# Attention rows 0 and 1: their scores made together in the step of row 2, side by side in the four score banks

## The reference

```python
q = (x_norm @ w_q.T).reshape(B, 512, 16, 32)      # 16 heads of 32
k, v = split(x_norm @ w_kv.T)                     # one key and one value head for all
q, k = rotary(q * scale), rotary(k * scale)
attn = einsum('bnih,bjh->bnij', q, k)             # causal: j <= i
out = einsum('bnij,bjd->bind', softmax(attn), v)
x = x + out.reshape(B, 512, 512) @ w_proj.T + b_proj
```

## Time and profile before

| | us |
|---|---|
| median of 3 runs | 2768.08 (2767.12 to 2768.15) |
| the profiled execution, its own time | 2771.93 |
| its span, first to last instruction | 2769.9 |
| mean granted TensorE clock | 0.994 |
| TensorE busy (share of the span) | 2718.5 (98%) |
| VectorE busy | 1852.0 (67%) |
| ScalarE busy | 1122.9 (41%) |
| GpSimd busy | 305.5 (11%) |

### The profile page before, as it was taken

The page is one execution under the profiler, slowest core; times in us unless marked ns, Lnnn a source line. Parts: engine busy times, 40 slices in busy tenths (PEclk is TensorE's granted clock), DMA queues, the critical chain, the costliest instruction groups (busy, mean ns, idle before and its releaser), DMA issues.

```text
span 2769.9 us, 41675 instructions
## 1 busy us (share of the span) xinstructions
PE 2718.5 (98%) x15520; PEld 2196.0 (79%) x15520; DVE 1852.0 (67%) x3533; ACT 1122.9 (41%) x2399; POOL 305.5 (11%) x316
## 2 busy tenths in 40 slices
PE   7999999999999999999999999999999999999998
PEld 5888888888888887677777768888888888888887
DVE  5667666765675667777777775667656766676555
ACT  3333333333333323777777774333333333333331
POOL 0000000000000004444444420000000000000000
PEclk9999999999999999999999999999999999999999
DMA  3210311131112111000000012211221032112100
GB/s 118 87 61 24 127 56 45 39 114 46 45 62 91 46 46 57 21 13 28 32 32 28 28 47 92 81 48 47 79 81 63 28 118 66 45 33 89 46 15 31
DMA packets 65069, 156.49 MB, mean 56 GB/s; under 512 B 6784, under 2 KB 7040, under 8 KB 64640
## 3 DMA queue, kind: packets, MB, share of 16 engines
q1 hardware_dynamic: 64896, 154.17, 16.5%
HBM read 128.97 MB, written 25.17 MB: 56 GB/s over the span
## 4 chain that ended last, share of the span: by engine, by line
PE 94%; DVE 4%; ACT 1%; POOL 1%; issue 1%; ACTq 0%; DVEq 0%; POOLq 0%
PE bank L371 50%; PE bank L392 24%; PE bank L1003 5%; PE bank L971 3%; PE bank L994 3%; PE bank L1018 3%; PE bank L1031 2%; PE bank L273 1%; DVE probs L1254 1%; PE bank L946 1%; PE bank L979 1%; POOL xnt_l L875 0%; DVE att L1273 0%; ACT hs_h L486 0%; DVE stats L243 0%
## 5 line engine op out<-in xcount | busy, mean ns | idle before, releaser
L371 PE MATMUL bank<-xnt_h,wgu_h 128*128 128x512 f32 x2048 | 803.0, 392 | 6.6 <-issue 3.7
L371 PE MATMUL bank<-xnt_h,wgu_l 128*128 128x512 f32 x2048 | 798.4, 390 | 0.0
L371 PE MATMUL bank<-xnt_l,wgu_h 128*128 128x512 f32 x2048 | 798.1, 390 | 0.0
L539 DVE TENSOR_TENSOR h<-bank,sg 128x512 f32<-128x512 f32 x256 | 176.8, 690 | 592.6 <-PE bank L371 577.0
L371 PEld LDWEIGHTS bank<-xnt_h,wgu_h 128*128 128x128 f32 x2048 | 385.1, 188 | 87.2 <-issue 5.1
L476 ACT ACTIVATE mag<-h 128x512 f32<-128x512 f32 x256 | 161.9, 633 | 713.5 <-DVE h L539 713.5
L371 PEld LDWEIGHTS bank<-xnt_h,wgu_l 128*128 128x128 f32 x2048 | 385.1, 188 | 80.9
L371 PEld LDWEIGHTS bank<-xnt_l,wgu_h 128*128 128x128 f32 x2048 | 385.3, 188 | 78.7
L392 PE MATMUL bank<-wd_h,hs_h 128*128 128x512 f32 x1024 | 399.6, 390 | 4.6 <-DVE hs_l L574 4.6
L392 PE MATMUL bank<-wd_l,hs_h 128*128 128x512 f32 x1024 | 399.3, 390 | 0.0
L392 PE MATMUL bank<-wd_h,hs_l 128*128 128x512 f32 x1024 | 399.2, 390 | 0.0
(11 more groups left out here) (109 smaller groups left out, 3195.8 us busy)
## 6 DMA issues: line engine op xcount, KB each, us to landing
raw_gu<-in_w_gu SPq DMA_DIRECT2D x128, 512.0 KB, 4.9
raw_d<-in_w_d SPq DMA_DIRECT2D x128, 256.0 KB, 2.6
x_mid<-x_sb SPq DMA_DIRECT2D x64, 256.0 KB, 2.0
x_sb<-x_mid SPq DMA_DIRECT2D x10, 1024.0 KB, 5.5
x_sb<-in_x SPq DMA_DIRECT2D x32, 256.0 KB, 4.8
out<-x_sb SPq DMA_DIRECT2D x32, 256.0 KB, 2.1
x_sb<-x_mid SPq DMA_DIRECT2D x24, 256.0 KB, 5.0
raw_q<-in_w_q SPq DMA_DIRECT2D x1, 1024.0 KB, 5.2
```

The costliest lines, as they stand in the source:

```text
L371: last = pe.matmul(ps, w[:, r, kind, k], xs[:, b, k], start=(i == 0), stop=(i == 3 * KD - 1))
L539: v.tensor_tensor(h[:, r], bank[UP + r % 2][:, :], sg[:, r % 2], ALU.mult).then_inc(h_done, 1)
```

## The change

Row 0's scores are no longer made in the step of row 1. They are made in the step of row 2, just ahead of those of row 1, and both lie in the same four banks at once: row 0 in columns 0 to 127, row 1 in columns 128 to 383. Row 1 does not wait for row 0 to be masked. One semaphore step of two announces both. The step of row 1 makes no scores. VectorE masks all heads of row 0 at the end of its step of row 2 (behind invert_sums) in place of the start of that step; ScalarE makes all four exponentials of row 0 at the end of its step of row 3, behind its two copies of turned blocks. The scores made before the first step (rows 0, 1 and 2 of the first head group) keep their order.

```diff
+            def columns(i):
+                first = P if i == 1 else 0
+                return slice(first, first + width(i))
 # TensorE
-                def scores(K):
+                def scores(K, beside=False):
...
-                    if K > 0:
+                    if K > 0 and not (beside and i == 1):
                         pe.wait_ge(masked, K * HG)
...
-                        last = pe.matmul(bank[SCORES + s][:, 0:width(i)], qt[rows, B % 2, hg, i * P:(i + 1) * P],
+                        last = pe.matmul(bank[SCORES + s][:, columns(i)], qt[rows, B % 2, hg, i * P:(i + 1) * P],
...
-                    last.then_inc(score_done, 1)
+                    if not beside:
+                        last.then_inc(score_done, 1)
+                    elif i == 1:
+                        last.then_inc(score_done, 2)
...
-                    if K + AHEAD < ALL:
+                    if i == 2 and K + AHEAD < ALL:
+                        scores(K + AHEAD - 1, beside=True)
+                        scores(K + AHEAD, beside=True)
+                    elif i != 1 and K + AHEAD < ALL:
                         scores(K + AHEAD)
 # ScalarE
-                    exps(K + 1, 2)
+                    if row_of(K) != 3:
+                        exps(K + 1, 2)
                     copy_turned(K, 0)
-                    exps(K + 1, 3)
+                    if row_of(K) != 3:
+                        exps(K + 1, 3)
                     if 2 in mine:
                         copy_turned(K, 2)
...
-                    exps(K + 2, 0)
-                    exps(K + 2, 1)
+                    if row_of(K) == 3:
+                        for s in range(HG):
+                            exps(K + 1, s)
+                    if row_of(K) != 2:
+                        exps(K + 2, 0)
+                        exps(K + 2, 1)
 # VectorE
-                    mask_scores(K + AHEAD - 1, (0, 1))
+                    if i != 2:
+                        mask_scores(K + AHEAD - 1, (0, 1))
                     if 1 in ON_VECTOR[i]:
                         copy_turned(K, 1)
-                    mask_scores(K + AHEAD - 1, (2, 3))
+                    if i != 2:
+                        mask_scores(K + AHEAD - 1, (2, 3))
...
-                    if k % TT == TT - 2:
+                    if i == 2:
                         invert_sums(K // TT)
+                        mask_scores(K + AHEAD - 1, range(HG))
```

More of the change, by code:

```diff
@@ L1253, in mask_scores @@
                     for s in heads:
-                        v.tensor_tensor_reduce(out=probs[:, K % 3, s, 0:w], in0=bank[SCORES + s][:, 0:w], in1=causal[:, S - w:S],
+                        v.tensor_tensor_reduce(out=probs[:, K % 3, s, 0:w], in0=bank[SCORES + s][:, columns(row_of(K))], in1=causal[:, S - w:S],
                                                scale=1.0, scalar=MASKED, op0=ALU.add, op1=ALU.min,
```

## The result

The changed kernel takes 2778.84 us (median of 5 runs, 2778.23 to 2779.37), the kernel before beside it 2767.12 (5 runs, 2763.04 to 2768.15). The ratio is 1.0043, 95% interval 1.0032 to 1.0055: slower by 11.7 us. The prediction was 2778 (2769 to 2788) with 0.73 for slower by over 0.2%.

A forecast was written before the change was run, and what follows sets the result against it. TensorE's queue bounds the kernel, with VectorE late in the row 3 step. Six middle batches +13.0, ends -1.3 and -3.5, a low-clock stretch +1.7: +9.9 us, 2781.8 profiled; less 3.9, 2778 us (2769 to 2788).

The forecast's parts named there:

- The row 3 step: From T, the start of its turns, to row 2's scores: 3.11 us, not 2.57, as VectorE masks row 0 first; +0.54.
- The price of the pair: Row 0's scores put ahead of row 1's on TensorE cost 0.22 us more in one group; upper bound 0.43.
- Rival (e): The merged score group costs 0.43 us, not 0.22: +6, 2784 us; inside the range, no chance of its own.
- The swallowed saving: In k = 5 to 6 the 0.52 us saved becomes TensorE's wait for the projection bank that VectorE frees.
- k = 9 to 12: Head group where VectorE's normalise and ScalarE's drain delay TensorE: +0.98 and +0.34 among terms summing to +0.89 us.
- Rival (d): ScalarE becomes the bound, row 1's last exponential 0.4 us before TensorE in k=8; each 0.1 beyond costs 1.5 us.
- k = 13 to 0: Head group ending each batch: -0.41 us saved, +0.16 from ScalarE's late row 0 exponentials in k=15; together -0.25.
- The ends: First and last batch: TensorE's waits for row 0's place in the banks go; -1.3, -3.5, and +1.7 for a low-clock stretch.
- The -4.4 of batch 0: Batch 0, from the start of k = 9 to the turns of k = 11: 5.73 us in place of 10.15.
- (a): Row 0's masks fit into VectorE's slack, so the row 3 step costs nothing: 2756 us; chance 0.08.
- (b): It comes out even: no loss in k=12, and the ends give more without a clock stretch: 2771 us; chance 0.19.
- (c): New or longer waits in k=1, 5, 12 let the clock fall: 2798 us, or 2788 for one per batch; chance 0.11.

The follow-up runs named there:

- run 5: Changed kernel with two extra 128-column VectorE copies among row 0's four masks, results unread: 2784.81 us, ratio to the kernel before 1.0073.
- run 8: Changed kernel with weigh placed between row 0's and row 1's score groups, same matmuls, waits and banks: 2785.05 us, ratio to the kernel before 1.0072.
- runs 1 to 3: Changed kernel with normalise ahead of row 0's masks (2779.45 us), with row 0's exponentials split around the copy of block 0 (2773.78), with both (2771.43).
- run 4: Kernel before with only ScalarE's new order of row 0's exponentials: 2783.51 us, ratio to the kernel before 1.0061.
- the two later ones: Second and third profiles of the unchanged kernel before: 2767.59 and 2766.62 us; attention stretch 573.3 and 573.1 us, against 575.8 in the first.
- runs 1 to 8: The follow-up variants timed in five rounds beside the kernel before, whose median was 2767.85 us beside the first four and 2767.18 beside the others.
- run 2: Changed kernel with row 0's exponentials on ScalarE split around the copy of block 0: 2773.78 us, ratio to the kernel before 1.0023.

## Why the prediction was right, and where it was not

**The row 3 step** is where the time goes, as predicted: T + 3.10 in the trace, 3.11 in the sum, and the extra copies of run 5 (0.41 of VectorE's queue) made each such step 0.40 longer. k = 1 to 4 and 5 to 8: +0.75 and +0.78 in batch 3 against +0.76.

**The price of the pair**: 0.22, measured 0.22, and run 8 shows that it hangs on the two groups being neighbours: parted, row 0's costs 0.21 more. The Trainium skill gives a reason (TensorEngine Tiling (Array Packing), Key Properties: a change of tiling mode drains TensorE, a change of tile does not). The 0.21 fit it, but no run parts the drain from another cost of starting a group, so the reason is argued and not shown. Rival (e) falls.

**The swallowed saving**: shown in the trace (0.80 of wait for the bank of the projection in k = 6), the start unchanged relative to the projection before.

**k = 9 to 12**: +0.97 in all in batch 3, summed as +0.89. The wait of k = 12 was a little longer than summed (0.43 of delay against 0.34). What runs 1 to 3 add is that these are two bounds in a row, and run 4 that ScalarE's new order by itself costs a middle batch as much as the whole change. Rival (d) was put as a risk of ScalarE in k = 8; the place where it bites is the drain of k = 12.

**k = 13 to 0**: -0.36 against -0.25. **A batch**: 2.15 on the mean against 2.16, six of them 12.9 against 13.0.

**The ends** were mis-sized, and by two errors that partly cancel. Against the first trace they gave 1.7 (batch 0) and 2.6 (batch 7), 4.3 in all, where the sum had 1.3 + 3.5 - 1.7 = 3.1. But 2.5 of that is the low stretch that the first trace had and the two later ones had not. The step that went wrong is "it lies 3.9 above the median ... so for the runs I say 2778": it took the 3.9 for something that both kernels keep. Most of it was a low stretch in the very place that the change rebuilds; the profiled run of after lies 0.5 above its median. With 2.5 less to win at the end the attention of after is 11.2 us longer than that of before, and the timed runs say 11.7, not the 9.9 of the sum. The landing within 1 us of the time is partly luck; the sum of the middle is not.

The -4.4 of batch 0 came out (T of k = 11 at 5.57 after the start of k = 9, summed as 5.73, where it was 10.14), but the 10.14 are those of an execution whose clock was low there. Run 4 has the same wait of 2.95 with the clock at 1.00, and there the same stretch takes 7.42: so 2.7 of the 4.6 are the low clock. So what the change wins at the ends depends on how often the clock falls in the kernel before. Of the 41 executions of it that were timed beside runs 1 to 8, the seven with a mean granted clock of 0.998 took 2762.39 to 2764.99, the thirty with 0.996 2765.65 to 2769.08. The five of after all had 0.998 and took 2778.23 to 2779.37. So against executions of before with the same mean clock the change costs about 15 us, not 11.7.

**Rivals**: (a) falls with run 5. (b) and (c) did not come: no low clock in batches 1 to 6. The stretch of 3.4 us that I added for k = 5 of batch 7 is there, behind 2.18 us of wait (0.79 over 8 us); from the first turn of k = 6 to that of k = 7 it is 4.70 in after and 3.31 in run 5, where the clock did not fall, so it cost 1.4 where I had put 1.7.

## What to carry to other kernels

A saving on the bound engine counts only where its next wait is not tied to something that does not move with it: here half of the head groups turned it into a wait for a bank. Work put in front of a queue costs its length less the slack behind it, and its full length where that queue already releases the bound engine without slack: here the first 0.85 us cost 0.54, the next 0.41 cost 0.40. So look for a wait that ends 0.06 us before its user starts. When two engines release the bound one in turn, measure each alone: moving the first showed nothing, moving both showed more than their sum. And try such a change place by place, not for the whole loop: in three of 31 places it was worth 5 us.

## What had not been expected of the hardware

The length of a stop of TensorE does not settle what the clock does behind it. Behind the same wait of 2.32 us at the same place of the program (k = 5 of batch 7) it fell in one execution (0.79 over the window) and stayed in two others (1.00). Behind 2.95 us in batch 0 it fell in all three traces of the kernel before (0.81 over the window in each) and stayed at 1.00 in the trace of run 4, which differs from it in ScalarE's order alone:

```profile
1154.77 0.50 PE L994 MATMUL bank<-kt,qt 32*128 32x128 f32 x8 [2.95 <-DVE nmax L1260]
...
1149.00:1166.50 17.50, 13.34 (x196) 9.66 (x191) 12.60 (x48) 15.43 (x50) 9.64 (x12) 1.00 0.01 2
```

Shorter stops do it too: behind 1.64 us in batch 0 (k = 14) it fell in the trace of run 2 (0.79 over 8 us) and stayed at 1.00 behind 1.65 us in after. What decides it was not tried. One profiled execution therefore does not give the price of such a stop.
